# Writing out the loops over groups of a fused group-norm and convolution kernel

## The chip, the cores and the metric

The kernel runs on one core of a Trainium2 chip. The metric is the time of one execution in microseconds on the device; lower is better. The core has five engines with instruction streams of their own: PE (matmul), DVE (vector), ACT (scalar), POOL (GpSimd) and SP (which only issues DMAs here). They meet through semaphores alone.

## The reference

The input `x` is one image of 16 channels of 2048 x 2048 float32. Two layers follow each other:

```python
x = x + L0_conv(_gn(x), weight)          # depthwise 6 x 11 convolution, lower triangle only
x = x + (_gn(x) + bias)                  # bias: a table of row minus column, per channel
```

`_gn` normalises each of 8 groups of 2 channels by its own mean and variance. The convolution reads and writes only the lower triangle (`tril`) of each channel. The bias table comes from a small three-layer network over the 4095 differences of row and column, computed once.

## The kernel before, in words

A group is two channels, 33.5 MB. The groups go through a pipeline of stages (`stage`, defined once for SP, ACT, DVE and POOL each). In stage `s`, part a takes the statistics of group `s` (loads into `abuf`, DVE line 743), part b convolves group `s - 1`, and part c finishes group `s - 2`: it scales, adds the bias and stores, partly from tiles kept in place (`kept`, line 889) and partly by streaming again through the four buffers of `ubuf` (lines 622 and 898, 1002). `stages` (lines 414 to 421) runs ten stages, 0 to 9. Stages 0, 1, 7, 8 and 9 are written out and leave out parts that don't apply; stages 2 to 6 are one body in a loop of the hardware, `eng.Fori(2, G - 1)` at line 417, executed five times by each of the four engines with a loop of its own. Stage 7 has parts a, b and c like the looped ones, but no first loads for a further group (`do_next` is False). Inside a stage, 90 tiles are written out by Python; an engine works in the order of these tiles, and that order is fixed.

PE's stream is separate. `group(g, before, after)` convolves the 90 tiles of a group in triples; most triples are in three near loops over tiles (lines 1100, 1104 and 1111), five triples of a group stand outside these. Groups 0 and 7 are called on their own; groups 1 to 6 are the body of `pe.Fori(1, G - 1)` at line 1119.

One tile goes through the engines like this. ACT normalises it into `xn` (line 558); POOL masks it where it touches the diagonal (line 970); PE transposes it into `psT` (line 1053); ACT rounds it to float16 in `XT` (line 573); DVE writes the remainder (line 715); POOL carries the border columns (lines 985 and 993); PE convolves with 36 matmuls into `psY` (line 1067); DVE adds the result to the input in place (lines 728 and 730), and ACT squares it for the second norm (line 595). Normalising runs four tiles ahead and `XT` two, with three buffers for each.

At a group's end there are two dependencies between all engines. DVE hands over the new group's first norm (lines 808 and 809, position 85 of the stage), which ACT waits for before it normalises tile 0 of the next group. And PE's `sum_results` (line 1093), placed before the first convolution of a group, waits for `stats2` part 0 on DVE (up to line 842), which needs all 90 tiles of the group before.

Semaphores count up through the whole run, so a wait's value grows with the group number `g`. In a loop `g` is a register, and each such value is computed by the engine's sequencer (ALU and fused register operations in the trace) before the wait; DMA addresses too. Outside a loop they are constants. SP's waits stand alone, each followed by a nop (`wait_alone`, line 378), and so do some of POOL's.

Of the kernel before, what the change touches and what calls it, by code (L numbers as in the profile page):

```python
# [25 lines left out]
def preact_conv_kernel(nc, x, wflip, w1, b1, w2, b2, w3, b3, out):  # L26
# [3 lines left out]
    AX = mybir.AxisListType  # L30

    _, CH, HH, WW = x.shape
    _, TR, TS = wflip.shape
    DIM = w2.shape[0]
    P, K, BW = 128, 4, 512
    CPG = 2
    G = CH // CPG
# [16 lines left out]
    def band_tiles(b):  # L54
# [11 lines left out]
    EDGES = [(n, BW * (b + 1) - STEP * (t + 1)) for n, (c, b, t) in enumerate(TILES)  # L66
             if b < NBAND - 1 and t == band_tiles(b) - 1 and BW * (b + 1) > STEP * (t + 1)]
    assert all(w <= XC - STEP % XC for _, w in EDGES)
    edges_before = lambda n: sum(e < n for e, _ in EDGES)
    NEDGE = len(EDGES)  # L70
# [173 lines left out]
    with ctx:  # L244
# [166 lines left out]
        block = ctx.enter_context(nc.Block())  # L411


        def stages(eng, stage):
            stage(0, True, False, False, True)
            stage(1, True, True, False, True)
            with eng.Fori(2, G - 1) as s:
                stage(s, True, True, True, True)
            stage(G - 1, True, True, True, False)
            stage(G, False, True, True, False)  # L420
            stage(G + 1, False, False, True, False)
# [3 lines left out]
        def _(sp):  # L425
# [87 lines left out]
            def load_bias(g, c):  # L513
# [5 lines left out]
                src = bass.AP(row.tensor, row.offset, [[K, P], [1, NV]])  # L519
                sp.dma_start(bias[:, :], src).then_inc(bias_loaded, 16)  # L520

            stages(sp, stage)


        @block.scalar
        def _(act):
# [105 lines left out]
            def stage(s, do_a, do_b, do_c, do_next):  # L632
                p, ga, gb, gc = plan(do_a, do_b, do_c, on_dve), s, s - 1, s - 2
                for n in range(NT):
# [29 lines left out]
                    if do_c:  # L664
# [14 lines left out]
                        for u in range(NU):  # L679
                            if p.u_store[u] == n:  # L680
                                store_stream(gc, u)

            stages(act, stage)

            for half_stored in kept_stored.values():
                act.wait_ge(half_stored, 16 * G)
# [7 lines left out]
        def _(dve):  # L694
# [170 lines left out]
            def build_weights(g, c):  # L865

                sc = wsc[:, bass.ds(chan(g, c), 1), 0]
                dve.wait_ge(w_loaded, 16 * K * (chan(g, c) + 1))
                wait(dve, convolved, NT * g if c else NT * (g - 1) + NTC)
                if isinstance(g, int) and g == 0 and c == 0:  # L870
                    dve.wait_ge(scale_chain, 6)
                nc.vector.tensor_copy(col(wback, c), wsc[:, bass.ds(chan(g, c), 1), 1]).then_inc(wback_ready, 1)
                nc.vector.tensor_scalar(wsplit[:, c, 0, :, :], wstage[:, :, :], sc, None, ALU.mult
                                        ).then_inc(w_hi_built, 1)
                dve.wait_ge(w_hi_built, chan(g, c) + 1)
                nc.vector.scalar_tensor_tensor(out=wsplit[:, c, 1, :, :], in0=wstage[:, :, :], scalar=sc,
                                               in1=wsplit[:, c, 0, :, :], op0=ALU.mult, op1=ALU.subtract
                                               ).then_inc(w_built, 1)
# [22 lines left out]
            def stage(s, do_a, do_b, do_c, do_next):  # L901
                p, ga, gb, gc = plan(do_a, do_b, do_c, on_dve), s, s - 1, s - 2
                for n in range(NT):
# [38 lines left out]
                            hand_over_norm(ga, gb if do_b else None)  # L942
                    if do_b and n == W_BUILD[1]:
                        build_weights(gb, 1)
            stages(dve, stage)


        @block.gpsimd
        def _(pool):
# [74 lines left out]
                            if p.u[u] == n and not on_dve[u]:  # L1024
                                add_bias(gc, u)

            stages(pool, stage)


        @block.tensor  # L1030
        def _(pe):
# [41 lines left out]
            def triple(N, c, ahead=NB3, results_of=None):  # L1073

                for i in range(NB3):
                    if i < ahead:
                        transpose(N + i + 2, (i + 2) % NB3)
                    if i == 0 and results_of is not None:
                        sum_results(results_of)
                    convolve(N + i, i, c)  # L1080
# [14 lines left out]
            def group(g, before, after):  # L1095

                first = NT * g
                pe.wait_ge(w_built, chan(g, 0) + 1)
                triple(first, 0, results_of=g - 1 if before else None)
                with pe.Fori(1, NTC // NB3) as j:  # L1100
                    triple(first + NB3 * j, 0)
                pe.wait_ge(w_built, chan(g, 1) + 1)
                triple(first + NTC, 1)
                with pe.Fori(NTC // NB3 + 1, SUM1[0] if after else 2 * NTC // NB3 - 1) as j:
                    triple(first + NB3 * j, 1)
                if after:
                    triple(first + NB3 * SUM1[0], 1)
                    sum_means(g + 1)
                    triple(first + NB3 * SUM1[1], 1)
                    sum_variances(g + 1)  # L1110
                    with pe.Fori(SUM1[1] + 1, 2 * NTC // NB3 - 1) as j:
                        triple(first + NB3 * j, 1)
# [3 lines left out]
            transpose(0, 0)  # L1116
            transpose(1, 1)
            group(0, False, True)
            with pe.Fori(1, G - 1) as g:
                triple(NT * g - NB3, 1)  # L1120
                group(g, True, True)
            triple(NT * (G - 1) - NB3, 1)
# [27 lines left out]
```

## Time and profile before

| | |
|---|---|
| Median of three runs | 2829.44 us (2829.42 to 2832.39) |
| The profiled execution | 2827.08 us, of which the span is 2825.3 us |
| Busy: PE, PE loads | 2010.8 us (71%), 1901.0 us (67%) |
| Busy: DVE, ACT, POOL | 2305.3 us (82%), 1665.3 us (59%), 1174.1 us (42%) |
| DMA | 916.67 MB, mean 324 GB/s |
| Granted PE clock, mean | 0.899 of full speed |

In the view by windows the busy times stand in the order PE, PEld (PE's weight loads), DVE, ACT, POOL, each with its instructions, and then the granted clock, the DMA share and GB/s. The span is the time from the first to the last recorded instruction. Busy time is the union of an engine's instructions; register, branch, semaphore and DMA-issuing instructions don't count as busy and are listed under the engine's name with a q (SPq, PEldq). The `XT` cast of line 573 runs once for each of the 720 tiles, so its start times give the time of each tile and group: the groups' first casts start at 146.3, 400.6, 727.2, 1056.9, 1392.5, 1724.8, 2058.3 and 2380.0 us.

### The profile page before, as it was taken

How to read it: one execution, taken by the hardware profiler on the slowest of the kernel's cores; microseconds unless marked ns; L12 is line 12 of the kernel's file. 1: busy time of each engine (PE TensorE's matmuls, PEld its weight loads, DVE VectorE, ACT ScalarE, POOL GpSimd, SP SyncE). 2: the span in 40 equal slices, each digit the busy share in tenths (PEclk: the TensorE clock that was granted, in tenths of full speed). 3: DMA queues.
4: the chain of work that ended last, by engine and by line, in shares of the span. 5: the costliest groups of instructions: out<-in, count | busy, mean ns of one | idle time of the engine just before them, and what ended most of it. 6: DMA issues, size and time to landing. Idle time of an engine off the chain costs nothing. (4 is left out here: it accounts for less than half of the span.)

```text
span 2825.3 us, 82231 instructions
## 1 busy us (share of the span) xinstructions
PE 2010.8 (71%) x28880; PEld 1901.0 (67%) x28880; DVE 2305.3 (82%) x4175; ACT 1665.3 (59%) x3051; POOL 1174.1 (42%) x1988
## 2 busy tenths in 40 slices
PE   4099887877678776878678786787777777888500
PEld 0098877767677776777577676787767776888500
DVE  6888888899788987899788997889888996958724
ACT  2067666756557565766556565675656656777621
POOL 1032225524435354453444344453543535555433
PEclk9999999999899998999789998899989999999855
DMA  8876849999799988999889997999989996879799
GB/s 253 305 252 216 295 161 354 381 349 343 264 395 357 358 330 306 387 343 365 294 329 389 338 347 272 383 386 337 340 308 386 359 374 244 313 266 332 286 342 340
DMA packets 319859, 916.67 MB, mean 324 GB/s; under 512 B 42864, under 2 KB 42864, under 8 KB 317520
## 3 DMA queue, kind: packets, MB, share of 16 engines
q1 hardware_dynamic: 203744, 595.03, 59.0%
q10 hardware_dynamic: 115840, 318.80, 29.2%
q8 instruction: 71, 1.16, 0.2%
q14 instruction: 204, 1.67, 0.2%
HBM read 594.18 MB, written 319.68 MB: 323 GB/s over the span
## 5 line engine op out<-in xcount | busy, mean ns | idle before, releaser
L1067 PEld LDWEIGHTS psY<-wsplit,XT 128*128 128x128 f16 x25920 | 1624.7, 102 | 354.7 <-DVE band L730 104.4
L1067 PE MATMUL psY<-wsplit,XT 128*128 128x168 f16 (+5 forms) x25920 | 1652.5, 224 | 287.3 <-DVE band L730 133.7
L573 ACT CAST XT<-psT 128x512 f16<-128x512 f32 x720 | 416.0, 578 | 581.5 <-PE psT L1053 263.3
L715 DVE TENSOR_TENSOR XT<-psT,XT 128x512 f16<-128x512 f32 x720 | 490.2, 681 | 310.9 <-ACT XT L573 310.0
L743 DVE BATCH_NORM_STATS2 entries<-abuf 128x6 f32<-128x512 f32 x928 | 586.9, 680 | 62.9 <-DMA abuf<-in_x 62.3
L970 POOL TENSOR_TENSOR xn<-xn,mask 128x512 f32<-128x512 f32 x336 | 417.7, 1243 | 524.3 <-ACT xn L558 440.9
L1053 PE MATMUL psT<-ident,xn 128*128 128x128 f32 x2880 | 484.9, 293 | 184.6 <-POOL xn L970 116.5
L1002 POOL TENSOR_TENSOR ubuf<-ubuf,bias 128x1024 f32<-128x1024 f32 x184 | 419.4, 2280 | 444.5 <-ACT ubuf L622 444.5
L993 POOL COPY halo<-XT 128x16 f16<-128x16 f16 x720 | 248.7, 345 | 609.2 <-DVE XT L715 595.0
L1053 PEld LDWEIGHTS psT<-ident,xn 128*128 128x128 f32 x2880 | 321.3, 148 | 198.0 <-POOL xn L970 113.3
L558 ACT ACTIVATE xn<-kept_c_band,normp 128x512 f32<-128x512 f32 (+2 forms) x496 | 398.5, 803 | 48.2 <-DMA kept_c_band<-in_x 24.2
L595 ACT ACTIVATE junk<-kept_c_band,cur 128x512 f32<-128x512 f32 (+2 forms) x464 | 311.8, 672 | 73.9 <-DVE kept_c_band L730 39.2
L730 DVE SCALAR_TENSOR_TENSOR kept_c_band<-psY,wback,kept_c_band 128x472 f32<-128x472 f32 (+3 forms) x496 | 343.8, 693 | 6.2
L889 DVE SCALAR_TENSOR_TENSOR kept_c_band<-kept_c_band,outp,bias 128x1024 f32<-128x1024 f32 x224 | 334.6, 1502 | 11.4 <-ACT bias L615 11.3
L622 ACT ACTIVATE ubuf<-ubuf,outp 128x1024 f32<-128x1024 f32 x184 | 209.5, 1140 | 221.9 <-DMA ubuf<-in_x 141.1
L898 DVE SCALAR_TENSOR_TENSOR ubuf<-ubuf,outp,bias 128x1024 f32<-128x1024 f32 x104 | 170.4, 1639 | 97.8 <-DMA ubuf<-in_x 63.6
L728 DVE TENSOR_TENSOR psY<-psY,mask 128x472 f32<-128x472 f32 (+2 forms) x336 | 203.5, 606 | 0.0
L558 ACT ACTIVATE xn<-band,normp 128x512 f32<-128x512 f32 (+1 forms) x224 | 174.3, 778 | 30.6 <-DVE normp L809 30.6
L985 POOL COPY XT<-halo 128x16 f16<-128x16 f16 x720 | 148.7, 207 | 58.1 <-PE psY L1067 53.9
L730 DVE SCALAR_TENSOR_TENSOR band<-psY,wback,band 128x472 f32<-128x472 f32 (+2 forms) x224 | 150.3, 671 | 5.6
L595 ACT ACTIVATE junk<-band,cur 128x512 f32<-128x512 f32 x192 | 132.1, 688 | 37.6 <-DVE band L730 32.3
L595 ACT ACTIVATION_READ_ACCUMULATOR junk<-kept_c_band,cur 128x1 f32 x464 | 87.0, 187 | 0.0
(77 smaller groups left out, 433.8 us busy)
## 6 DMA issues: line engine op xcount, KB each, us to landing
abuf<-in_x SPq DMA_DIRECT2D x464, 512.0 KB, 7.3
out<-ubuf ACTq DMA_DIRECT2D x288, 512.0 KB, 5.9
kept_c_band<-in_x SPq DMA_DIRECT2D x224, 512.0 KB, 7.8
out<-kept_c_band ACTq DMA_DIRECT2D x224, 512.0 KB, 7.2
ubuf<-in_x SPq DMA_DIRECT2D x192, 512.0 KB, 6.7
band<-in_x SPq DMA_DIRECT2D x48, 1024.0 KB, 8.6
out<-band ACTq DMA_DIRECT2D x48, 1024.0 KB, 9.7
ubuf<-out SPq DMA_DIRECT2D x96, 512.0 KB, 7.1
```

The source lines that it names most:

```text
L558: last = nc.scalar.activation(to[:, :, 0:whole, :], slot(c, b)[:, :, x0:x0 + XC * whole].rearrange("p k (i c) -> p k i c", c=XC), ACT.Iden ...
L573: nc.scalar.copy(XT[:, n % NB3, 0, :, 2:P + 2], psT[n % NB3][:, :, :]).then_inc(hi_ready, 1)
L595: nc.scalar.activation(junk[:, 0:nr * (c1 - c0)].rearrange("p (r c) -> p r c", r=nr), slot(c, b)[:, r:r + nr, BW * q + c0:BW * q + c1], AC ...
L715: nc.vector.tensor_tensor(XT[:, n % NB3, 1, :, 2:P + 2], psT[n % NB3][:, :, :], XT[:, n % NB3, 0, :, 2:P + 2], ALU.subtract).then_inc(lo_r ...
L730: nc.vector.scalar_tensor_tensor(out=xs, in0=y, scalar=col(wback, c), in1=xs, op0=ALU.mult, op1=ALU.add, accum_out=sums[:, n:n + 1]).then_ ...
L743: last = nc.vector.bn_stats(entries[:, e, :], row(q, r))
L889: nc.vector.scalar_tensor_tensor(out=v, in0=v, scalar=col(outp, 0), in1=bias_at(blk, nr // 2 * h, nr // 2), op0=ALU.mult, op1=ALU.add).the ...
L970: nc.gpsimd.tensor_tensor(v, v, m, ALU.mult).then_inc(xn_ready, 1)
L993: nc.gpsimd.tensor_copy(halo[:, t, :, :, :], XT[:, n % NB3, :, :, P:P + 2]).then_inc(halo_out, 1)
L1002: nc.gpsimd.tensor_tensor(v, v, bias_at(STREAM[u]), ALU.add).then_inc(u_added, 1)
L1053: last = nc.tensor.transpose(psT[m][:, i, :], xn[:, m, i, :, :].rearrange("p k c -> p (k c)"), ident[:, :])
L1067: last = nc.tensor.matmul(psY[m][:, 0:rows, o + lo_c:o + hi_c], XT[:, m, xp, i, 2 - sh:2 - sh + P], wsplit[:, c, wp, K * sh:K * sh + rows, ...
```

## The change

The loops over groups are replaced by Python loops. The same bodies are issued five times on SP, ACT, DVE and POOL and six times on PE. The group number is then a Python integer, so waits and addresses are constants (in PE's near loops over tiles a register remains). The number and order of loads, waits and arithmetic instructions on data stay. Where the code asks `isinstance(s, int)`, the cases concerned are stages 0 and 1, which were written out before too; a wait whose value is an integer of zero or less is left out, which touches only early groups.

```diff
-        def stages(eng, stage):
+        def stages(stage):
             stage(0, True, False, False, True)
             stage(1, True, True, False, True)
-            with eng.Fori(2, G - 1) as s:
+            for s in range(2, G - 1):
                 stage(s, True, True, True, True)
             stage(G - 1, True, True, True, False)
             stage(G, False, True, True, False)
...
-            stages(sp, stage)
+            stages(stage)
...
             group(0, False, True)
-            with pe.Fori(1, G - 1) as g:
+            for g in range(1, G - 1):
                 triple(NT * g - NB3, 1)
                 group(g, True, True)
             triple(NT * (G - 1) - NB3, 1)
```

ACT, DVE and POOL call `stages` in the same way as SP.

## Rows read from the trace of the kernel before

**Rows 1.** The page, busy time, share of the span and instructions by engine.
```profile
PE 2010.8 (71%) x28880; PEld 1901.0 (67%) x28880; DVE 2305.3 (82%) x4175; ACT 1665.3 (59%) x3051; POOL 1174.1 (42%) x1988
```

**Rows 2.** By windows, seven heads: start:end, length, busy by engine, clock, DMA.
```profile
395.30:415.70 20.40, 12.86 (x161) 12.21 (x159) 12.52 (x33) 12.69 (x31) 7.76 (x18) 0.77 0.63 223
718.90:748.20 29.30, 15.73 (x171) 15.37 (x172) 15.04 (x35) 12.86 (x30) 8.03 (x18) 0.65 0.82 285
1051.40:1079.70 28.30, 13.78 (x168) 13.51 (x167) 15.42 (x35) 12.79 (x30) 8.81 (x18) 0.70 0.78 278
1386.10:1415.70 29.60, 16.07 (x169) 15.66 (x170) 15.30 (x35) 12.86 (x30) 8.80 (x18) 0.62 0.82 290
1719.20:1748.50 29.30, 15.10 (x172) 14.79 (x173) 15.06 (x35) 12.89 (x31) 8.55 (x18) 0.68 0.81 282
2051.70:2076.20 24.50, 15.48 (x170) 15.13 (x171) 15.03 (x35) 12.87 (x31) 8.31 (x18) 0.65 0.92 333
2374.60:2396.50 21.90, 11.47 (x141) 10.92 (x139) 12.61 (x31) 12.74 (x30) 8.51 (x18) 0.77 0.90 324
```

**Rows 3.** By windows, tiles 3 to 74: two looped stages, then the written-out.
```profile
748.20:1000.40 252.20, 199.33 (x2907) 190.02 (x2905) 224.95 (x406) 158.61 (x287) 110.93 (x190) 0.93 0.95 356
...
1415.70:1666.50 250.80, 197.59 (x2889) 188.08 (x2888) 224.37 (x406) 158.52 (x287) 109.51 (x190) 0.93 0.95 356
...
2076.20:2326.30 250.10, 199.52 (x2903) 190.58 (x2901) 223.96 (x406) 158.09 (x288) 109.42 (x190) 0.93 0.96 358
```

**Rows 4.** By source line, 1060 to 1070 us: duration ns min/median/max, start.
```profile
L417 SPq COMPARE_BRANCH  x1: 54/54/54, 1061.2 to 1061.2; - x1
...
L417 DVEq COMPARE_BRANCH  x1: 72/72/72, 1064.9 to 1064.9; - x1
```

**Rows 5.** Timeline of DVE: start, length, instruction [idle before, releaser].
```profile
1071.20 0.69 DVE L715 TENSOR_TENSOR XT<-psT,XT 128x512 f16<-128x512 f32 x1 [5.70 <-ACT XT L573]
...
2067.77 0.69 DVE L715 TENSOR_TENSOR XT<-psT,XT 128x512 f16<-128x512 f32 x1 [0.47 <-ACT XT L573]
```

**Rows 6.** Waits of the whole span: us in total, times, longest.
```profile
ACT junk L595 <- issue: 20.9, 4, 5.3
```

**Rows 7.** Timeline of SP's queue, after a taken branch and in the exit.
```profile
1071.65 1.12 SPq L474 DMA_DIRECT2D ubuf<-out  x2
...
2063.98 0.93 SPq L474 DMA_DIRECT2D ubuf<-out  x2
```

**Rows 8.** By source line, whole span: PE's far and near branches.
```profile
L1119 PEldq COMPARE_BRANCH  x6: 76/5728/6668, 715.0 to 2372.0; - x6
...
L1100 PEldq COMPARE_BRANCH  x112: 76/208/234, 165.1 to 2528.5; - x112
```

**Rows 9.** Timeline of PE, after a taken far branch and after none.
```profile
2052.59 1.09 PE L1053 MATMUL psT<-ident,xn 128*128 128x128 f32 x4 [5.52 <-DVE XT L715]
2053.47 3.81 PE L1067 MATMUL psY<-wsplit,XT 128*128 128x148 f16 x36
...
2373.04 2.12 PE L1067 MATMUL psY<-wsplit,XT 128*128 128x148 f16 x36
2377.04 0.63 PE L1053 MATMUL psT<-ident,xn 128*128 128x128 f32 x4 [1.88 <-POOL xn L970]
```

**Rows 10.** By windows, hand-over to first `XT` cast of the new group.
```profile
718.90:727.20 8.30, 5.61 (x46) 5.52 (x47) 5.32 (x12) 5.15 (x11) 2.80 (x6) 0.60 0.85 290
1051.40:1056.90 5.50, 5.50 (x69) 5.49 (x68) 4.23 (x12) 5.02 (x12) 2.81 (x6) 0.69 0.69 218
...
2051.70:2058.30 6.60, 5.71 (x47) 5.61 (x48) 4.53 (x12) 5.12 (x12) 2.80 (x6) 0.50 0.64 198
2374.60:2380.00 5.40, 3.29 (x55) 3.13 (x53) 4.28 (x12) 4.93 (x11) 2.80 (x6) 1.00 0.84 296
```

**Rows 11.** The page, DMA queues: packets, MB, share of 16 engines.
```profile
q14 instruction: 204, 1.67, 0.2%
```

**Rows 12.** Waits in group 7, 2374 to 2661 us.
```profile
PEld psY L1067 <- issue: 13.4, 14, 2.2
```

More of the change, by code:

```diff
@@ L681, in stage @@
                                 store_stream(gc, u)
-            stages(act, stage)
+            stages(stage)
             for half_stored in kept_stored.values():
@@ L944, in stage @@
                         build_weights(gb, 1)
-            stages(dve, stage)
+            stages(stage)
         @block.gpsimd
@@ L1025, in stage @@
                                 add_bias(gc, u)
-            stages(pool, stage)
+            stages(stage)
         @block.tensor
```

## The prediction

> **What bounds the kernel now.** I read the page first. DVE is busy for 82% of the span, and PE, ACT and POOL have slack [rows 1]; the 16 DMA engines are 95 to 96% busy in the long middle stretches [rows 3]. So no single engine is a wall. The order of work decides, and the edit touches one thing in it: how each engine gets from one stage to the next, and how it knows its wait values. I therefore cut the span where one group's normalisation is handed over (the DVE copy of line 808, once in each of the eight groups, at 395.3, 718.9, ... 2374.6) and measured each piece in the view by windows. A "head" runs from that copy to the start of the fourth `XT` cast of the new group (line 573). It contains the PE loop's far branch, the stage branch of the other four engines, and the global sums of `sum_results`/`stats2`.
>
> Seven heads exist [rows 2]. The first (395.3) lies before any backward branch, but its stage still stores nothing and moves few bytes. The next four contain the branch back to line 417 and last 29.3, 28.3, 29.6 and 29.3 us, 116.5 us in all. The sixth (2051.7) is the exit of the same loop: the same code runs through the branch untaken, and the full load of statistics, streams and stores surrounds it. It takes 24.5. The seventh takes 21.9, with less to load. Between heads, the six stretches from the fourth tile to tile 74 are alike whatever the branch did before them: 250.1 to 252.2 us, of which the two longest-apart looped ones and the written-out one are shown [rows 3]. So a stall in a head is not made good later. This is what makes it worth money although the DMA share looks like a limit.
>
> **Part 1: the backward branch at line 417 goes.** It is executed five times on SP, ACT, POOL and DVE; the branch instruction itself takes 0.05 us on SP and 0.07 on DVE [rows 4]. That isn't its cost. After the branch of 1064.9 DVE starts nothing until 1071.20, 5.70 us idle; at the exit, branch 2066.7, the next tile comes 0.47 us after the last work [rows 4, 5]. ACT shows the same with nothing else to blame: it waits for "issue" before line 595, 20.9 us over 4 times, the number of taken branches [rows 6]. SP's first transfer after its branch of 1061.2 is issued at 1071.65, while in the exit (branch 2063.0) it is issued at 2063.98 [rows 4, 7]. All four stop nearly together, so their stalls of 5 to 6 us overlap and count once per group; SP's comes first and lasts longest, and delays the `ubuf` loads that ACT and DVE wait for. Written out, the next stage simply follows, as at 2063.
>
> How short does a head become? From below: 21.9 us, that of the seventh. From above: 24.5, that of the sixth, which still holds PE's branch (part 2). A third bound comes from bytes. Rate times length gives 8.35, 7.87, 8.58 and 8.26 MB for the four heads and 8.16 for the sixth [rows 2]; their mean, 8.27 MB, at the 356 GB/s that a full stretch sustains [rows 3] takes 23.2 us. I take 23.4, near the sixth and what the DMA engines allow, rather than the lighter seventh. Saved: 116.5 - 4 x 23.4 = 22.9 us.
>
> **Part 2: PE's outer branch at line 1119 goes.** PE sits in it for 5.7 us in the median, against 0.21 for the near branches of line 1100, which stay [rows 8]. But it mostly stalls where it would soon wait anyway. In the sixth head PE starts again at 2052.59 after 5.52 us idle, with transposes of 1.09 us instead of 0.63 and a convolution of 3.81 instead of 2.12; without a taken branch (2372) it does that tile early and then waits for the mask until 2377.04 [rows 9]. From the hand-over to the first cast of the new group it takes 8.3, 5.5, 6.4, 5.6 and 6.6 us where PE branches, and 5.3 or 5.4 where it does not; the granted clock is 0.50 to 0.69 against 1.00, that is, mostly or partly at the 1.2 GHz level against 2.4 GHz [rows 10]. So the branch costs 6.5 - 5.35 = 1.1 us per group on the path, not 5.7. Four of the five are inside the 22.9 already. The fifth is the sixth head: 24.5 - 23.4 = 1.1 us. What hides the other 4.6 us is DVE's work before the hand-over, which does not depend on PE's branch; if that cover were gone, up to 5 x 4.6 = 23 us more would come.
>
> **Part 3: constant waits and addresses.** The five looped stages spend register instructions on the sequencers ahead of waits and DMAs; stages 0, 1 and 7 to 9 don't. They run beside the datapaths: they matter only when the queue before an engine is empty. The price is the difference between tiles 3 to 74 of the five looped stages (252.2 at most, 250.8 at least, mean 251.3) and of the written-out stage (250.1), with the same work [rows 3]: 1.2 us against the mean, 0.7 against the nearest. I take 0.8 a stage, 4 us for five; the ends are 0 and 6. PE's own near loops keep their register values, so nothing changes there. SP's DMA addresses no longer come from registers, but SP mostly waits for buffers, so I price this at nothing; if that cover is missing it is already within the 6.
>
> **What the change adds.** Only code: four more copies of a stage on four engines and five of a group on PE. A looped stage is already read in straight through, being far longer than the stretch a branch can reach without a stall, so what is fetched stays about the same. The larger of the two instruction queues carries 1.67 MB in this run, 0.2% of the DMA engines' time [rows 11]. I price it at nothing; the bound from above is the third rival.
>
> Two rules of the Trainium skill bear on parts 1 and 2. "Advanced Engine Details and Errata", section "Control Flow Timing", gives about 108 ns for a compare-and-branch; by it the branches of line 417 would be worth 0.4 us along one engine, and the change nothing. The rows above disagree: untaken or near, the trace agrees within a factor of two; taken and far, the stall is some fifty times as long. "Runtime: NRT & Kernel Launch", section "Instruction fetch mechanics", says that a taken branch beyond the held pages must wait for a fetch. By it every taken far branch costs and no other, and that is how the five executions divide here.
>
> **Sum.** 22.9 + 1.1 + 4.0 = 28.0 us. The profiled execution took 2827.08 us (span 2825.3 and 1.8 around it), so it would become 2799.1. The median of the runs is 2829.44, 2.4 above the profiled one: 2801.5, or 1.0% less.
>
> **Rivals.**
> 1. *DMA takes half of it.* The sixth head already has a DMA share of 0.92 against 0.78 to 0.82 in the four before it [rows 2], and DVE's line 898 waits there for `ubuf` loads that SP can now ask for only as fast as stores finish. If heads end at 26.3, halfway, and constants bring 1, the gain is 4 x 2.8 + 1 = 12: 2817. Against it: the byte count, and the same stretches after long and short heads. 0.10.
> 2. *Everything at its better end.* Heads of 21.0 (between 20.4 and 21.9, the first and seventh), in the sixth too, and 1.2 us a stage: 4 x 8.1 + 3.5 + 6 = 42: 2787. Against it: both those heads move fewer bytes or carry fewer statistics. 0.10.
> 3. *Slower: fetches in PE's written-out code.* PE goes through instructions fastest, 36 loads and 36 matmuls in 2.12 us [rows 9]. If its straight code behind each near loop had to wait for a fetch once groups no longer share one place, each would cost what a far branch costs, 5.7 us. With three such places in each of six groups that is 103 us less the 28: 2904. From five such stalls on the path the gain is gone. Against it: groups 0 and 7 are written out already with the same near loops, and in group 7 no wait that the convolution's loads put down to "issue" is over 2.2 us [rows 12]. The skill's page on the runtime says of straight code that its fetches are hidden by the pace of the sequencer; it sides with the rows. 0.03.
> 4. *No change.* The far stalls are not the branch's but that of the place (the sums need results of all engines there), and would stay: 2829. Against it: the exit runs the same place with 0.47 us instead of 5.70. 0.03.
>
> **How the numbers follow.** The forecast, 2801.5, has 0.74. Its own ends are 2829.4 - 22.9 - 1.1 = 2805 without constants, 2809 with heads of 24.5 (18.5 + 0 + 2), and 2794 with heads of 22.4. To hold 8 in 10 the range reaches partly into rivals 1 and 2: 2788 to 2815. Under 0.2% is 5.7 us, about what a measurement here can tell from none. Faster by more: 0.74 + 0.10 + 0.10 = 0.94. Within: 0.03, rival 4. Slower: 0.03, rival 3.
>
> **What would show it.** Part 1: no idle stretch of 5 us on DVE or ACT at stage starts, no ACT "issue" wait before line 595, and heads of 23 to 24.5 us in groups 2 to 6. Part 2: no branch record of line 1119, PE's clock near 1.00 just after the hand-over, and 5.3 us from there to the first cast. Part 3: 250 us for tiles 3 to 74, no register instructions on ACT, DVE and POOL. The prediction is wrong if heads stay at 28 us (the stall was of the place), if stretches between heads grow past 253 us (the DMA engines take it back), or if PE shows new idle time of 5 us put down to "issue" within its written-out groups.

## The result, and the profile after

| | before | after |
|---|---|---|
| Median | 2829.43 us (4 runs, 2826.88 to 2832.39) | 2789.83 us (4 runs, 2786.79 to 2794.84) |
| Profiled span | 2825.3 us | 2790.1 us |
| Instructions recorded | 82231 | 76859 |
| Granted PE clock, mean | 0.899 | 0.907 |

The ratio is 0.9861, 95% interval 0.9845 to 0.9877: 1.4% faster, 39.6 us by the medians and 35.2 by the two profiled spans. The forecast was 2801.5 us (range 2788 to 2815), a gain of 28.

The page of the changed kernel: busy time by engine, and the two instruction queues (packets, MB, share of 16 DMA engines). It answers to [rows 1, 11].

```profile
PE 1993.1 (71%) x28880; PEld 1881.5 (67%) x28880; DVE 2296.2 (82%) x4175; ACT 1661.3 (60%) x3051; POOL 1167.8 (42%) x1988
...
q8 instruction: 60, 0.98, 0.1%
q14 instruction: 126, 1.03, 0.1%
```

DVE is busy for 9 us less, PE for 18; on DVE the other 26 of the 35 us are idle time that went. Less code was fetched, not more: 2.01 MB in the two queues against 2.83.

The heads, cut as before from DVE's line 808 to the fourth `XT` cast (view by windows: start:end, length, busy of PE, PEld, DVE, ACT and POOL, clock, DMA share, GB/s). These five answer to the second to sixth row of [rows 2]: the four that held the branch, and the exit.

```profile
716.60:739.70 23.10, 11.82 (x131) 11.53 (x132) 14.95 (x35) 12.82 (x31) 8.11 (x18) 0.66 0.93 335
1043.70:1067.10 23.40, 12.35 (x131) 12.05 (x132) 14.94 (x35) 12.90 (x31) 8.06 (x18) 0.65 0.94 342
1368.20:1391.60 23.40, 11.88 (x130) 11.58 (x131) 14.99 (x35) 12.75 (x31) 8.46 (x18) 0.71 0.91 317
1691.80:1715.20 23.40, 12.29 (x129) 12.00 (x130) 14.96 (x35) 12.78 (x31) 8.07 (x18) 0.71 0.95 336
2016.50:2039.80 23.30, 12.17 (x129) 11.88 (x130) 15.04 (x35) 12.73 (x30) 8.10 (x18) 0.65 0.94 335
```

They last 23.1 to 23.4 us where they lasted 28.3 to 29.6 and 24.5, with DMA shares of 0.91 to 0.95. They also carry less: rate times length gives 7.74, 8.00, 7.42 and 7.86 MB for the first four, mean 7.76, where the four before had 8.27. Tiles 3 to 74 of groups 1 to 6, in the same view, answer to [rows 3]:

```profile
413.80:661.50 247.70, 196.39 (x2903) 187.06 (x2902) 223.72 (x406) 158.09 (x288) 109.22 (x190) 0.94 0.94 356
739.60:989.80 250.20, 197.00 (x2891) 187.52 (x2889) 224.65 (x406) 158.18 (x288) 109.67 (x190) 0.94 0.96 362
1067.00:1315.00 248.00, 198.52 (x2903) 189.40 (x2901) 223.26 (x406) 157.99 (x287) 110.02 (x190) 0.92 0.96 363
1391.60:1640.50 248.90, 197.16 (x2892) 187.64 (x2890) 223.34 (x406) 157.95 (x287) 109.17 (x190) 0.94 0.96 362
1715.10:1963.80 248.70, 195.68 (x2892) 186.15 (x2890) 222.60 (x406) 158.07 (x288) 109.22 (x190) 0.94 0.96 362
2039.80:2291.80 252.00, 201.15 (x2901) 192.09 (x2899) 223.25 (x406) 158.13 (x287) 109.38 (x190) 0.91 0.95 358
```

The first five are the stages that were looped: 247.7, 250.2, 248.0, 248.9 and 248.7 us, mean 248.7 against 251.3. The sixth was constant before on SP, ACT, DVE and POOL, and its code there has not changed; it went from 250.1 to 252.0. So one stretch scatters by 2 us from program to program, and only means of several say something.

SP's queue and DVE's timeline at the place of [rows 5, 7], where stage 4 begins (start, length, instruction, idle before):

```profile
1052.90 0.34 SPq L520 DMA_DIRECT2D bias<-bias_scratch  x1
1054.11 0.99 SPq L474 DMA_DIRECT2D ubuf<-out  x2
```

```profile
1058.30 0.69 DVE L715 TENSOR_TENSOR XT<-psT,XT 128x512 f16<-128x512 f32 x1 [0.45 <-ACT XT L573]
```

SP issues its first load of the stage (line 474) 1.2 us after the last of the stage before (line 520), and DVE's 5.70 us of idle time has become 0.45, as in the exit before.

The two spans account for the gain like this, hand-over to hand-over: before group 1's hand-over 1.9 us, group 1 0.4, groups 2 to 5 together 32.9 (heads 23.2, tiles 3 to 74 9.7, the rest nothing), group 6 -1.8, after the last hand-over 1.8. In group 1, tiles 3 to 74 became 3.3 us shorter and the stretch from there to the next hand-over 2.8 us longer (52.3 to 55.1), so what a middle saves is not all kept: from tile 3 to the next hand-over the five looped groups took 303.9 us in the mean before and 301.9 after, 2.0 us less and not 2.6.

### The profile page after: what moved, and what is told of

Its sections match the earlier page's. It is cut to its first block and busy times, and to the rows that moved or that the text cites. A ratio compares the mean times of both kernels' runs of the same rounds, so it can differ in the third digit from the quotient of the medians.

```text
span 2790.1 us, 76859 instructions
## 1 busy us (share of the span) xinstructions
PE 1993.1 (71%) x28880; PEld 1881.5 (67%) x28880; DVE 2296.2 (82%) x4175; ACT 1661.3 (60%) x3051; POOL 1167.8 (42%) x1988
## 3 DMA queue, kind: packets, MB, share of 16 engines
q1 hardware_dynamic: 203744, 595.03, 59.6%
q14 instruction: 126, 1.03, 0.1%
## 5 line engine op out<-in xcount | busy, mean ns | idle before, releaser
L1067 PEld LDWEIGHTS psY<-wsplit,XT 128*128 128x128 f16 x25920 | 1608.0, 102 | 366.1 <-issue 123.2
L1067 PE MATMUL psY<-wsplit,XT 128*128 128x168 f16 (+5 forms) x25920 | 1635.9, 223 | 296.4 <-DVE band L730 130.9
L970 POOL TENSOR_TENSOR xn<-xn,mask 128x512 f32<-128x512 f32 x336 | 411.1, 1224 | 499.7 <-ACT xn L558 437.1
L993 POOL COPY halo<-XT 128x16 f16<-128x16 f16 x720 | 241.5, 335 | 615.2 <-DVE XT L715 600.7
L898 DVE SCALAR_TENSOR_TENSOR ubuf<-ubuf,outp,bias 128x1024 f32<-128x1024 f32 x104 | 159.2, 1532 | 105.9 <-DMA ubuf<-in_x 71.5
L985 POOL COPY XT<-halo 128x16 f16<-128x16 f16 x720 | 156.5, 217 | 59.1 <-PE psY L1067 54.3
```

Of the source, the lines that this page charges most:

```text
L970: nc.gpsimd.tensor_tensor(v, v, m, ALU.mult).then_inc(xn_ready, 1)
L993: nc.gpsimd.tensor_copy(halo[:, t, :, :, :], XT[:, n % NB3, :, :, P:P + 2]).then_inc(halo_out, 1)
L1067: last = nc.tensor.matmul(psY[m][:, 0:rows, o + lo_c:o + hi_c], XT[:, m, xp, i, 2 - sh:2 - sh + P], wsplit[:, c, wp, K * sh:K * sh + rows, ...
```

## The experiments

Times are medians, and each ratio is to the kernel before on the same chip in the same job. In those jobs the kernel before had medians of 2826.8, 2831.4 and 2829.0 us, with single runs from 2817.9 to 2842.4, so a few us between two of the kernels are not shown by their medians alone; the means of heads (groups 2 to 5) and middles (groups 1 to 5, tiles 3 to 74) come from the profiled run of each and are set beside them.

| kernel | median us | ratio (95% interval) | head | middle |
|---|---|---|---|---|
| before | 2829.4 | 1 | 29.1 | 251.3 |
| changed | 2789.8 | 0.9861 (0.9845 to 0.9877) | 23.3 | 248.7 |
| e1 hinted loops | 2815.9 | 0.9963 (0.9945 to 0.9981) | 26.3 | 251.5 |
| e5 hinted loops, POOL written out | 2817.2 | 0.9943 (0.9923 to 0.9963) | 25.1 | 252.4 |
| e2 one trip | 2793.5 | 0.9879 (0.9839 to 0.9920) | 23.8 | 249.5 |
| e3 PE looped | 2797.4 | 0.9891 (0.9853 to 0.9928) | 24.5 | 250.0 |
| e8 PE looped and hinted | 2795.4 | 0.9865 (0.9829 to 0.9902) | 24.4 | 249.9 |
| e6 POOL looped | 2794.2 | 0.9863 (0.9829 to 0.9896) | 23.0 | 249.7 |
| e9 SP looped | 2805.5 | 0.9914 (0.9879 to 0.9949) | 23.4 | 250.8 |
| e11 DVE looped | 2813.3 | 0.9943 (0.9919 to 0.9967) | 27.3 | 249.4 |
| e10 ACT looped | 2819.2 | 0.9965 (0.9945 to 0.9985) | 28.9 | 250.3 |
| e4 no loops at all | 2820.0 | 0.9968 (0.9950 to 0.9986) | 23.3 | 252.5 |
| e7 the same, other wait order | 2815.0 | 0.9944 (0.9925 to 0.9963) | 22.4 | 252.9 |
| e12 extra copies | 2795.1 | 0.9881 (0.9837 to 0.9924) | 22.7 | 249.7 |

The means of heads and middles come from one profiled execution each. For e9 that execution took 2797.5 us, 8 us less than the kernel's median.

My theory at first was that of the prediction: the far branches' stalls carry the gain, constants little. The rival was that the register work carries it.

### Loops kept, stalls taken away (e1)

The kernel before, with a prefetch hint for the closing branch at the head of each iteration:

```diff
-            with eng.Fori(2, G - 1) as s:
+            with nc.Fori(2, G - 1, engines=bass.OrderedEngineSet([eng.engine]), hint_back_edge=True) as s:
...
-            with pe.Fori(1, G - 1) as g:
+            with nc.Fori(1, G - 1, engines=bass.OrderedEngineSet([pe.engine]), hint_back_edge=True) as g:
```

> The kernel before with all loops over groups kept, and each far loop armed with a prefetch hint for its closing branch at the head of every iteration. Register values and the branches stay; only the wait for code at the branch should go. Theory (the heads are lost to the far branches' stall): heads of groups 2 to 6 fall from 28.3-29.6 to 23.4-24.5 us, tiles 3 to 74 stay at 251.3, time about 2829 - 24 = 2805. Rival (the time goes to register arithmetic, the branch only marks the place): heads stay above 28, time 2826 to 2831.

Line 417 by source, around the second branch (duration ns min/median/max, start): the branch, and the first instruction of the next iteration, which is the hint. ACT needs 0.4 us from one to the other, POOL 5.6.

```profile
L417 ACTq COMPARE_BRANCH  x1: 63/63/63, 1063.2 to 1063.2; - x1
...
L417 POOLq COMPARE_BRANCH  x1: 54/54/54, 1063.2 to 1063.2; - x1
...
L417 ACTq BRANCH_PREFETCH_HINT  x1: 52/52/52, 1063.6 to 1063.6; - x1
...
L417 POOLq BRANCH_PREFETCH_HINT  x1: 38/38/38, 1068.8 to 1068.8; - x1
```

PE's far branch, which took 5728 ns in the median in [rows 8]:

```profile
L1119 PEldq COMPARE_BRANCH  x6: 85/339/373, 712.2 to 2360.5; - x6
```

SP took 0.5 us, DVE 0.5. So the hint took away all far stalls but POOL's (5.1 to 5.8 us at the four branches; where the branch is not taken, 3.4 us pass at this place too before POOL's next instruction of line 382). Yet only 0.37% was gained, and the heads of groups 2 to 5 are uneven:

```profile
717.10:745.60 28.50, 13.54 (x130) 13.12 (x131) 15.93 (x35) 12.78 (x31) 8.78 (x18) 0.64 0.83 300
1049.00:1075.70 26.70, 13.05 (x129) 12.67 (x130) 16.86 (x35) 12.80 (x30) 8.77 (x18) 0.64 0.89 314
1379.50:1403.70 24.20, 13.46 (x130) 13.04 (x131) 15.73 (x35) 12.81 (x31) 8.78 (x18) 0.67 0.95 342
1709.70:1735.40 25.70, 12.20 (x129) 11.82 (x130) 15.93 (x35) 12.82 (x30) 7.78 (x18) 0.67 0.91 317
```

28.5, 26.7, 24.2 and 25.7 us save 11.4 us in all, and the middles nothing. The waits of the first of these heads, and of the same head in the changed kernel, say where its length comes from:

```profile
DVE ubuf L898 <- DMA ubuf<-in_x: 5.3, 2, 3.9
```

```profile
DVE ubuf L898 <- DMA ubuf<-in_x: 1.4, 1, 1.4
```

DVE waits at line 898 (as numbered in the kernel before) for `ubuf` loads, 5.3, 2.6, 1.2 and 2.5 us in the four heads of e1 and 3.7, 2.8, 1.4 and 3.3 in those of e5 below, against 1.4 to 1.8 in the changed kernel; the long heads are those with the long wait. In the first head that wait ends at 728.9, ahead of the branches of SP, ACT and DVE (730.9, 733.0 and 734.6). Neither the theory (2805) nor the rival (2826 or more) had it right: taking the stalls away brings 11 to 14 us, half of what I expected, and the remaining 22 to 26 us (to e2 in the same job, and to the changed kernel) need something else.

### Is it POOL's remaining stall? (e5, e6)

e5 is e1 with POOL's stages written out; e6 is the changed kernel with POOL's loop put back, unhinted.

```diff
-            with eng.Fori(2, G - 1) as s:
-                stage(s, True, True, True, True)
+            if eng.engine == nc.gpsimd.engine:
+                with eng.Fori(2, G - 1) as s:
+                    stage(s, True, True, True, True)
+            else:
+                for s in range(2, G - 1):
+                    stage(s, True, True, True, True)
```

(e6; e5 has the two bodies exchanged, with the hint in the loop of the others.)

> As e1_hinted_loops, with the loop over stages on POOL alone written out. In e1 the hint shortened the far branches of SP, ACT, DVE and PE to 0.3-0.6 us, but POOL still stopped for 5.1 to 5.8 us at each, and the heads fell only to 24.2-28.5. Theory (POOL's stall alone held the heads up, constants are worth about 2 us a group): heads 23.3 to 24.5, tiles 3 to 74 at 251, time about 10 us under e1_hinted_loops, so 2803 to 2808. Rival (something else of the loop holds the heads, such as register work at their start): heads stay at 26, time as e1.

> The changed kernel with the loop over stages put back on POOL alone, without a hint. Theory (POOL's stall of 5-6 us is enough to hold a head up by itself): four heads of 25 to 28 us, tiles 3 to 74 at 249, 2790 + 4 x 3 = 2802. Rival (POOL has slack, 42% busy, and its stall is hidden): heads 23.4, 2790.

e5 is no faster than e1 by its median, and e6 no slower than the changed kernel by more than the scatter (heads 23.0 us). By its ratio e5 is 0.2% faster than e1, which their intervals don't tell from nothing. By e6 POOL's stall is hidden, and the theory that it alone held up the heads in e1 fell.

### One engine looped at a time (e9, e10, e11, e3, e8)

The same edit with another engine in the condition; for e3 only PE's loop is put back, and e8 hints it.

> The changed kernel with the loop over stages put back on SP alone (far branch without a hint, DMA addresses and wait values in registers). Theory (SP stops first and its stall also hits the next block, so the `ubuf` loads of the head are late): heads 25 to 27 us, tiles 3 to 74 at 249 to 250, 2800. Rival A (SP's register work before each DMA is what the middle lost): tiles 3 to 74 at 251 to 252 too, 2810. Rival B (hidden like POOL's, e6): heads 23.4, 2790 to 2795.

> The changed kernel with the loop over stages put back on ACT alone. ACT casts each transposed tile, so its stall of 5 to 6 us stops PE and DVE. Theory: heads 26 to 28 us, tiles 3 to 74 at 250 to 251 because ACT computes the most register values of the datapath engines (some 240 a stage), 2808. Rival (the slack of an engine that is 60% busy takes it): heads 24, tiles 3 to 74 at 249, 2793.

> The changed kernel with the loop over stages put back on DVE alone, the busiest engine. Theory: its stall of 5.5 to 6.2 us lies whole on the path, heads 28 us, tiles 3 to 74 at 249 to 250, 2810. Rival (the four stalls are worth the whole only together, since each engine alone can be caught up with by the others' lead): heads 24 to 25, 2795.

Heads of ACT looped, then DVE looped, then SP looped, by windows: for each the shortest and the longest of its four.

```profile
722.10:750.30 28.20, 13.47 (x130) 13.07 (x130) 15.70 (x35) 12.80 (x31) 8.79 (x18) 0.65 0.95 343
1713.70:1744.20 30.50, 12.38 (x130) 12.09 (x131) 15.01 (x35) 12.78 (x30) 8.82 (x18) 0.66 0.91 324
```

```profile
716.10:744.20 28.10, 12.81 (x130) 12.52 (x131) 14.96 (x35) 12.74 (x31) 8.19 (x18) 0.64 0.96 347
1375.60:1402.10 26.50, 12.33 (x129) 12.04 (x130) 14.97 (x35) 12.76 (x31) 8.63 (x18) 0.69 0.95 354
```

```profile
718.80:742.40 23.60, 12.11 (x130) 11.81 (x131) 14.96 (x35) 12.75 (x31) 8.46 (x18) 0.71 0.80 286
1698.90:1722.20 23.30, 11.77 (x129) 11.48 (x130) 15.01 (x35) 12.73 (x30) 8.40 (x18) 0.71 0.77 270
```

ACT alone gives heads of 28.2 to 30.5 us: the whole of what all five engines together gave (28.3 to 29.6). DVE alone gives 26.5 to 28.1. SP alone gives 23.3 to 23.6, that is, nothing. So the stalls do overlap and count once, as the prediction had it; but it is ACT's and DVE's that count. SP's comes first and I had called it the longest, and it costs the heads nothing. By the medians ACT looped costs 29 us of the 39.6, DVE 24, SP 16, and the sum is far over the whole. Each of these has the stall and the register work of its engine together.

SP shows a second thing: its heads are as short as in the changed kernel and it still costs 0.5%. Its middles are 250.8 us.

> The changed kernel with PE's loop over groups put back (line 1119); SP, ACT, DVE and POOL stay written out. Theory (PE's far branch costs 1.1 us a group on the path, five times, and its register values nothing): 2795, tiles 3 to 74 at 248.7, hand-over to first cast 6.5 instead of 5.4 us. Rival (PE's constants made the middle shorter): tiles 3 to 74 at 251.3 and time about 2808.

> The changed kernel with PE's loop over groups put back and its far branch hinted, so PE keeps register waits in the five triples outside the near loops. Theory (PE's branch with a hint takes 0.3 us and is hidden, register waits on PE cost nothing): 2788 to 2793, the same as the changed kernel. Rival (PE's constants gave the middle 1 us a group, e3 against the changed kernel): 2796.

PE looped costs 7.6 us against the changed kernel's median and 4 against e2, whose code is equivalent (below); the expected 5.5 lies within. But not where it was expected: from the hand-over to the first cast, e3 takes 5.9, 5.5, 5.4, 5.4 and 6.3 us where PE branches, mean 5.7 and not 6.5, so the branch costs 0.3 us a group there. Its heads of 22.9 to 25.5 us follow DVE's wait for `ubuf` loads at line 898 instead (3.6, 2.7, 0.3 and 2.9 us). Hinted the loop costs about as much, 2 us less. Both have middles of 250.0, 1.3 above the changed kernel and 0.5 above e2; whether register waits on PE cost anything is not settled by this.

### What register addresses cost (found in e9 and e10)

In [rows 2, 3] I looked at datapaths only. The sequencer's records hold the answer. Line 454 issues the `abuf` loads. Before, by source, 748 to 2051 us:

```profile
L454 SPq FUSED_REGOPS  x227: 37/37/65, 765.7 to 2044.4; - x114
L454 SPq MOVE abuf<-in_x x227: 29/29/37, 765.8 to 2044.5; - x114
L454 SPq DMA_DIRECT2D abuf<-in_x x227: 331/333/2547, 765.8 to 2044.5; - x114
```

After, 740 to 2016 us:

```profile
L454 SPq DMA_DIRECT2D abuf<-in_x x227: 327/386/1500, 757.1 to 2008.3; - x114
```

In the looped stage each load is preceded by a fused register operation and a move that build its address, and they come after the wait of line 382 has ended, since the waits stand ahead of them in the stream. On ACT the fused operation itself carries the wait. Two timelines show it for a store behind DVE's line 889, first before, then after:

```profile
1154.77 1.28 DVE L889 SCALAR_TENSOR_TENSOR kept_c_band<-kept_c_band,outp,bias 128x1024 f32<-128x1024 f32 x1
1156.21 0.34 ACTq L610 DMA_DIRECT2D out<-kept_c_band  x1
```

```profile
1146.06 1.27 DVE L889 SCALAR_TENSOR_TENSOR kept_c_band<-kept_c_band,outp,bias 128x1024 f32<-128x1024 f32 x1
...
1147.36 0.34 ACTq L610 DMA_DIRECT2D out<-kept_c_band  x1
```

DVE ends at 1156.05 and the store is issued at 1156.21, 0.16 us later; in the changed kernel DVE ends at 1147.33 and the store is issued at 1147.36, 0.03 us later. Over the middle of the run the medians are:

| kernel | SP: wait to DMA issue | ACT: producer's end to store issue |
|---|---|---|
| before | 0.174 us | 0.159 us |
| e1, e5 | 0.171 | 0.160, 0.159 |
| e9 SP looped | 0.174 | 0.033 |
| e10 ACT looped | 0.028 | 0.160 |
| changed, e11 | 0.028 | 0.032, 0.033 |

(Taken from the sequencers' records between 748 and 2051 us: 516 to 528 DMAs on SP, 134 to 163 stores on ACT, those issued within 0.6 us of their producer's end.)

These delays lie in rings: a buffer of `ubuf` is loaded, finished, stored, and loaded again when the store has landed. There are 36 streams for each group and four buffers, so nine turns, and each turn has one load and one store: 9 x (0.146 + 0.127) = 2.5 us a group, an estimate from the rows above, if every turn is on the path, which no run shows. Measured are 2.6 us in the middles, and 2.0 from tile 3 to the next hand-over. That they come so near is luck, given the scatter; but the direction is borne out: the five kernels in which neither SP nor ACT has registers (changed, e2, e6, e11, e12) have middles of 248.7 to 249.7 us, those where one has (e9, e10) 250.8 and 250.3, those where both have (before, e1, e5) 251.3 to 252.4. With PE's registers alone (e3, e8) they are 250.0 and 249.9. Counted from tile 3 to the next hand-over, the first five have 301.9 to 303.1 us, e9 and e10 303.3 and 302.8, and the last three 303.9 to 305.0: registers on both engines still stand out, on one alone they don't.

### Does PE's code fetch cost anything? (e4, e7, e12)

Here the near loops of PE are written out too, which the change left alone. It was the extreme of the prediction's third rival.

```diff
-                with pe.Fori(1, NTC // NB3) as j:
+                for j in range(1, NTC // NB3):
                     triple(first + NB3 * j, 0)
```

(and the two loops after it alike)

> The changed kernel with PE's near loops over tiles written out too, so that no engine has a loop and PE reads some 60000 instructions in a straight line. Theory (near branches and PE's register values are hidden, straight code is fetched in time): 2790, within 3 us. Rival (PE outruns the fetch of straight code, as feared in the third rival of the prediction): new idle time of 5 us in PE's records many times, time above 2830.

30 us slower than the changed kernel. By the two profiled spans 19 of the 30 are in the five middles, 5 behind the last hand-over, and none in the heads. In PE's stream no gap of over 0.3 us stands ahead of an instruction that carries no wait, but for the same two as in the changed kernel (one at the start, one after the last convolution). So the rival's mechanism, PE waiting for its own code, is not what happened. Two other things differ. One is the wait order:

> As e4_no_loops_at_all (no engine loops, 2820), with the waits ahead of PE's transposes and convolutions in another order, so that the wait that mostly ends last is carried by the weight load itself, as in the looped form, and not by an instruction of the sequencer before it. Theory (e4 lost its 27 us because with constants the late wait sits in the sequencer: mask to transpose 0.115 us in the median against 0.052, last release to convolution 0.124 against 0.063): these return to 0.05 and 0.06, tiles 3 to 74 to 249, time 2788 to 2795. Rival (e4 lost it to the fetch of PE's code, 3.8 MB instead of 1.0): no change, 2815 to 2825.

The edit moves the waits for `xn_ready` and `evicted` ahead of the others in `transpose` and `convolve`. The two medians did return, from 0.115 to 0.053 us (mask's end to transpose, 61 cases) and from 0.124 to 0.061 (to the convolution, 220 cases), but the time fell only to 2815.0. So a late wait in the sequencer instead of on the instruction costs 0.06 us each. In all that is 5 us by the medians and 7 by the ratios, which these intervals don't tell from nothing.

The other is fetched code. PE's instruction queue in e4, to be read against q8 in the page above:

```profile
q8 instruction: 231, 3.78, 0.5%
```

171 packets more, 16 KB each, and each took 1.03 us on its DMA engine. The loads of `ubuf` land later, first in the changed kernel, then in e4 (issues, KB, median us to landing):

```profile
ubuf<-in_x SPq DMA_DIRECT2D x192, 512.0 KB, 6.4
```

```profile
ubuf<-in_x SPq DMA_DIRECT2D x192, 512.0 KB, 7.2
```

And ACT, which waits for them in order, waits longer: changed kernel, e4, e7 (us in total, times, longest).

```profile
ACT ubuf L622 <- DMA ubuf<-in_x: 140.1, 46, 6.8
```

```profile
ACT ubuf L622 <- DMA ubuf<-in_x: 164.8, 49, 8.1
```

```profile
ACT ubuf L622 <- DMA ubuf<-in_x: 172.7, 51, 7.8
```

25 and 33 us more of waiting go with 30 and 25 us more of time. But this wait doesn't follow the time elsewhere: it is 141.1 us in the kernel before, which is 40 us slower than the changed one, and 152.8 in e9. That the fetches are what delays the loads is argued from this and not shown. The attempt to show it missed:

> The changed kernel with 184 copies of 16 KB added, DRAM to DRAM, one contiguous row each, issued by SP every fourth tile; their result is not used. PE's written-out code in e4 fetched 171 more blocks of 16 KB, each 1.03 us on one DMA engine, and was 27 us slower than the changed kernel, of which the order of waits explained only 5 (e7). Theory (a block fetch holds one of the 16 DMA engines for 1 us, and every load that needs all 16 waits for it, so fetched blocks cost time in stretches that are 95% full): 2805 to 2820, tiles 3 to 74 at 251 to 253. Rival (such small traffic, 3 MB of 916, is lost among the rest): 2790 to 2796.

```diff
+                    if do_b and n % 4 == 0:
+                        k = (s - 1) * 23 + n // 4
+                        sp.dma_start(extra_dram[k:k + 1, :], x[0, 0, 2 * k:2 * k + 2, :] ...).then_inc(extra, 16)
```

2795.1 us, the rival's value. But the copies did not do what a fetch does. Queue q1 had 203744 packets before the edit:

```profile
q1 hardware_dynamic: 209632, 598.06, 59.7%
```

5888 packets more for 184 copies are 32 for each: by their sizes in the trace, 16 of 1 KB, each 0.046 us, and 16 of 4 bytes. A copy was spread out, a fetch is one packet of 16 KB. So e12 shows only that 3 MB of small packets cost nothing that these runs can tell; the question of long packets stays open.

### One trip (e2)

> The code is written out as in the changed kernel, but each copy of a stage or group sits in a loop of its own with one trip, so that group numbers are in registers again and no far branch is taken. Theory (constants are worth what tiles 3 to 74 lost, 251.3 to 248.7 us a group): heads 23.1 to 24.5, tiles 3 to 74 at 251, time 2803 to 2807. Rival (straight code itself, not the constants, shortens the middle): tiles 3 to 74 at 248.7, time 2790.

It was to keep the registers with no far branch. But outside PE's near loops the executed code holds only the loops' own counters, five additions and five branches on each engine (six on PE), and every wait and address in it is a constant: 76937 instructions against 76859. A loop of one trip was resolved. So it is nearly the changed kernel a second time, and useful as such: 2793.5 us, heads 23.8, middles 249.5 show how far two builds of the same work differ.

## Why the prediction was right, and where not

The direction was right, and the time lies within the range, 1.8 us from its lower end: the gain is 39.6 us where 28 were forecast. By steps:

**Part 1, far branches on four engines.** Forecast: heads of 23.4, 22.9 us saved. Measured: 23.1 to 23.4, 23.2 us saved. The size holds, but that it holds so closely is luck. The bound by bytes (23.2 us) took 8.27 MB at 356 GB/s; the heads carry 7.76 MB at 317 to 342 GB/s, and by their own bytes the same bound would be 21.8. The reason given is only half right. e1 took the stalls away and got 11.4 us from the same heads. The sixth head, on which I leaned, had not only no taken branch but also constants behind it, since stage 7 was written out; I read a difference of two causes as one. It also scatters: with the same stage 7 it is 24.5 us before, 23.5 in e1 and 26.2 in e5. And the order of the engines was wrong: SP's early stall is hidden (e9), ACT's and DVE's each suffice (e10, e11). e1's and e5's heads stay at 24 to 28 us because DVE waits for `ubuf` loads at line 898. Whether register work makes these loads late is open: e2, which has none on SP, ACT, DVE and POOL, has one head of 25.4 us with 3.5 us of the same wait.

**Part 2, PE's far branch.** Forecast 1.1 us a group, five times. The hand-over to the first cast takes 5.4 to 5.5 us in all groups after, as forecast from [rows 10], and putting the loop back costs 4 to 8 us (e3). But with all other loops gone the branch adds 0.3 us there and not 1.1, and e8, without its stall, costs nearly as much. The size can't be told from the scatter, and that the stall makes it is not shown.

**Part 3, constants.** This is the term that was mis-sized: 0.8 us a stage, 4 in all, was forecast; the five middles lost 13.1 us, of which 10.0 are left when the stretches behind them are counted. With the part of the heads that e1 leaves, what is not the stall is worth some 22 to 26 us of the 39.6, if the stalls are taken away first. That split hangs on the order, since the loop on ACT alone lengthens the heads by as much as all loops together (e10), and that constants make all of it is argued and not shown; no run has constants with the stalls kept on all engines. The step that failed is "they run beside the datapaths". It is true of wait values, which are computed ahead of the wait. It is not of DMA addresses on SP and ACT, which are built behind it (0.174 us from wait to issue against 0.028 on SP); I priced SP's at nothing because SP "mostly waits for buffers", when exactly then an instruction behind the wait delays the load. A second fault was to take the price from one written-out stage (250.1 us) whose code the change doesn't touch and which reads 247.3 to 252.0 in kernels with the same code for it.

**Code added.** Priced at nothing, and the fetched code even fell, from 2.83 to 2.01 MB. The rule from the Trainium skill, "Runtime: NRT & Kernel Launch", section "Instruction fetch mechanics", that a taken branch beyond the held pages waits for a fetch, is borne out: unhinted, 5.2 to 6.2 us from the branch to the next iteration's first instruction on SP, ACT and DVE, and 4.7 to 6.7 in the branch on PE. Its advice in the same section that kernels prefer full unrolling where possible holds for the four engines and not for PE here: e4 is 30 us slower than the changed kernel.

**Rivals.** The first (DMA takes half) did not come in the changed kernel: DMA shares rose to 0.91 to 0.95 and the heads fell all the same. Its mechanism is what e1 shows, though: with the stalls gone and the registers kept, DVE waits at line 898 and the heads end at 26.3 us in the mean, the rival's own value. The second (2787) is the nearest to the measured 2789.8 in value, but not in mechanism, as the heads are 23.3 and not 21.0. The third and fourth did not come.

## What to carry to other kernels

Where a hardware loop's body is long, compare its executions with its exit: the same code with the branch untaken shows what the stall costs, and putting one engine's loop back at a time shows whose stall it is; they do not add up. In a kernel bound by turning buffers round, look at what stands between a wait and the DMA behind it: addresses from registers added 0.13 to 0.15 us to each here, an estimated 2.5 us a group if each turn counts. And write out what runs far, not what runs near: a short loop over tiles on PE was worth keeping.

## What the runs showed of the hardware that I had not expected

- A prefetch hint cut the far branch to 0.3 to 0.6 us on PE, SP, ACT and DVE; on POOL the same hint left 5.1 to 5.8 us. Without a taken branch 3.4 us pass there too, which fits that POOL's stall is hidden.
- A 16 KB contiguous copy from DRAM to DRAM went out as 16 packets of 1 KB (0.046 us each) and 16 of 4 bytes, while PE's code travels in packets of 16 KB that take 1.03 us each.
- With constants, of several waits ahead of a PE instruction the first in the program was carried by the weight load and the others by an instruction before it; which one is late makes 0.06 us (0.115 us from the mask's end to the transpose in e4, 0.053 in e7).
